# A fused two-layer attention and FFN kernel: the third norm moved into the down products, queries for four sequences at once, the second attention in another order

## The reference

```python
x = x + L0_xattn(layernorm(x), ctx, ctx, ...)   # gated attention, 4 heads
x = x + L0_ffn(layernorm(x), w_gate, w_up, w_down)  # quantized FFN, 768 wide
x = x + L1_xattn(layernorm(x), ctx, ctx, w_q, b_q, w_k, b_k, w_v, b_v, w_o, b_o)  # 16 heads of 16
x = x + L1_ffn(layernorm(x), w_router, wi, wo)  # top-2 of 8 experts, 1024 wide, capacity 160
```

```python
q = (query @ w_q.T + b_q);  k, v likewise from ctx
scores = q @ k.T / sqrt(16)          # per head, 128 x 128
out = softmax(scores) @ v            # per head
out = out @ w_o.T + b_o
```

## Time and profile before

| | us |
|---|---|
| median of 3 runs | 653.67 |
| lowest and highest | 650.80, 655.14 |
| the profiled execution, its own time | 650.85 |
| its span | 649.1 |
| PE busy in it | 547.4 (84%) |
| DVE busy | 385.5 (59%) |
| ACT busy | 297.5 (46%) |
| POOL busy | 153.2 (24%) |

### The profile page before, as it was taken

How to read it: one execution, slowest core, us unless ns; L and a number is a source line. 1 busy time by engine, 2 the same in 40 slices (tenths; PEclk the granted TensorE clock), 3 DMA queues, 4 the chain that set the end, 5 groups by cost and what they waited for, 6 DMA issues and landing times.

```text
span 649.1 us, 10190 instructions
## 1 busy us (share of the span) xinstructions
PE 547.4 (84%) x3542; PEld 385.3 (59%) x3542; DVE 385.5 (59%) x931; ACT 297.5 (46%) x584; POOL 153.2 (24%) x218
## 2 busy tenths in 40 slices
PE   1869999899899103999799999988489999999994
PEld 1548866644344003788576666656277777777773
DVE  5666789644599798676677777774723213332111
ACT  1536587433699696000487777773211222112220
POOL 2725442000000000000322222202014443444531
PEclk9979999899899755999999999998789999999998
DMA  7800000000000000700000000001303544545310
GB/s 232 264 1 3 2 0 1 2 0 1 0 0 0 1 1 0 259 0 0 1 2 2 33 8 28 23 13 55 112 22 111 186 129 152 178 122 186 116 51 21
DMA packets 30152, 37.57 MB, mean 58 GB/s; under 512 B 6560, under 2 KB 25888, under 8 KB 30112
## 3 DMA queue, kind: packets, MB, share of 16 engines
q1 hardware_dynamic: 27040, 29.07, 13.6%
q0 software_dynamic: 3072, 7.95, 4.1%
HBM read 30.14 MB, written 6.88 MB: 57 GB/s over the span
## 4 chain that ended last, share of the span: by engine, by line
PE 67%; DVE 15%; ACT 9%; issue 5%; SPq 1%; DMA 1%; DVEq 0%; POOL 0%; ACTq 0%; POOLq 0%
PE pA L1631 11%; PE pB L1649 9%; PE pC L1441 6%; PE pC L1482 4%; PE pB L1491 3%; PE pA L1476 3%; PE pB L1464 3%; PE pB L1551 3%; PE pA L1403 3%; ACT arena L570 2%; PE pC L1642 2%; PE pC L1315 2%; PE pC L1403 2%; PE pB L1403 2%; DVE arena L1039 2%
## 5 line engine op out<-in xcount | busy, mean ns | idle before, releaser
L1631 PE MATMUL pA<-arena 128*128 128x320 f32 x256 | 72.2, 436 | 0.9 <-ACT arena L733 0.9
L452 POOL TENSOR_TENSOR arena<-KT,par 128x256 f32<-128x256 f32 x32 | 18.9, 613 | 221.5 <-PE pC L1441 201.5
L740 ACT ACTIVATE arena<-pA 128x320 f32<-128x320 f32 x64 | 28.0, 437 | 73.8 <-PE pA L1631 73.8
L1631 PEld LDWEIGHTS pA<-arena 128*128 128x128 f32 x256 | 48.0, 190 | 19.5 <-ACT arena L733 1.0
L1649 PE MATMUL pB<-arena 128*128 128x256 f32 x256 | 59.3, 385 | 0.0
L1649 PEld LDWEIGHTS pB<-arena 128*128 128x128 f32 x256 | 47.4, 190 | 9.4 <-issue 3.1
L972 DVE TENSOR_REDUCE am<-arena 128x1 f32<-128x512 f32 (+1 forms) x48 | 32.0, 680 | 23.7 <-ACT arena L607 23.7
L1104 DVE TENSOR_REDUCE rm<-pA 128x16 f32<-128x2048 f32 x16 | 36.7, 2291 | 14.8 <-PE pA L1476 14.8
L1226 PE MATMUL pB<-ident 128*128 128x128 f32 x120 | 18.6, 323 | 31.0 <-DVE arena L1039 31.0
L692 ACT ACTIVATE arena<-pC 128x512 f32<-128x512 f32 x64 | 38.2, 597 | 9.6 <-PE pC L1482 8.5
L1441 PE MATMUL pC<-wdnT,XIT 128*128 128x256 f32 x192 | 41.7, 380 | 0.9 <-DVE XIT L1059 0.9
(11 more groups left out here) (289 smaller groups left out, 1173.8 us busy)
## 6 DMA issues: line engine op xcount, KB each, us to landing
arena<-in_L_ffn_wi SPq DMA_DIRECT2D x8, 1024.0 KB, 5.1
arena<-in_L_ffn_wo SPq DMA_DIRECT2D x8, 1024.0 KB, 6.0
X<-in_x SPq DMA_DIRECT2D x4, 512.0 KB, 5.9
arena<-in_ctx SPq DMA_DIRECT2D x4, 512.0 KB, 5.8
out<-X SPq DMA_DIRECT2D x4, 512.0 KB, 2.9
token_rows<-arena SPq DMA_DIRECT2D x4, 512.0 KB, 4.0
arena<-in_L_ffn_w_up SPq DMA_DIRECT2D x1, 768.0 KB, 9.2
arena<-in_L_ffn_w_gate SPq DMA_DIRECT2D x1, 768.0 KB, 10.7
```

Of the source, the lines that this page charges most:

```text
L740: nc.scalar.activation(HT[:, u, f, :], ps[2 + f % 2][:, 0:ROWS], ACT.Relu).then_inc(s["h_relu"], 1)
L1631: last = mm(ps[2 + f % 2][:, 0:ROWS], WI[:, u, k, f * P:(f + 1) * P], XET[:, u, k, :], start=(k == 0), stop=(k == KD - 1))
```

## The change

- **Norm in the down stage.** DVE runs moments for sequences 0 to 7 at its turn t = 9 of the down stage, for 8 to 11 at t = 13, and norms two sequences a turn from t = 10 on, into the four buffers that `pair` names. The last four sequences' moments are cut in two: `variances` behind the stage, `inverse_roots` in the attention.
- **Queries for four.** `c_turn(p)` transposes a pair of sequences into one bank; `c_query(c, e)` makes half e of the queries of four sequences in two matmuls of 512 columns; `q_out(c, e)` puts them into XIT, where all queries stay. c_turn 0 to 3 and the first queries stand among the down products, the rest ahead of and in the attention's first turns. OT moves out of XIT.
- **New order.** In PE's turn t come a_out(t-3), o_turn(t-2), turn_3(t-1), scores1(t+1), turn_0(t), a_turn(t-2), values(t-1) in one block, turn_1(t), turn_2(t). Transposes 0, 1 and o_turn use one bank of pC, 2 and 3 the other. ACT and DVE are written out in matching orders, and the keep_busy of this stage is gone.
- POOL's `split_keys` starts when o_int has done eight sequences, and the tables that POOL writes to XIT wait for the last scores.

```diff
+        XC4 = [F3[:, o:o + 1024].rearrange("p (k n) -> p k n", k=KD) for o in (512, 2048)]
...
-        OT = tiles(XIT, 0)
+        OT = view(HALF, 2, FT, P)
...
-        BANK_OF = (1, 1, 0, 1)
+        BANK_OF = (1, 1, 0, 0)
+        QUERY_BANK = ((2, 3), (6, 7), (4, 4), (4, 6))
+        TURN_BANK = (4, 5, 4, 5, 4, 5, 6, 6)
...
                 if isinstance(b, int) and b == 0:
-                    pool.wait_ge(s["down_done"], NB)
+                    pool.wait_ge(s["oi_ready"], 8)
...
+            pool.wait_ge(s["scores"], NB)
...
+            def xt_copy(p):
+                act.wait_ge(s["c_tr"], p + 1)
+                c = p // 2
+                if c >= 2:
+                    act.wait_ge(s["c_q"], 2 * c - 2)
+                nc.scalar.activation(XC4[c % 2][:, :, (p % 2) * 2 * P:(p % 2 + 1) * 2 * P], ps[TURN_BANK[p]][:, :].rearrange("p (k n) -> p k n", k=KD), ACT.Copy).then_inc(s["c_xt"], 1)
+            def q_out(c, e):
+                act.wait_ge(s["c_q"], 2 * c + e + 1)
+                nc.scalar.activation(XITv[:, e, 512 * c:512 * c + 512], ps[QUERY_BANK[c][e]][:, :], ACT.Identity, scale=0.25, bias=bq[:, e:e + 1]).then_inc(s["qt_ready"], 1)
+            rsqrt(3, 8)
+            xt_copy(0)
+            xt_copy(1)
+            rsqrt(4, 4, 8)
+            xt_copy(2)
+            q_out(0, 0)
+            q_out(0, 1)
+            xt_copy(3)
...
             def pt_copy(b, u, g):
+                if g == 0:
+                    free_after(act, s["pv_done"], b)
                 act.wait_ge(s["pt_tr"], b * 4 + g + 1)
...
-            steps(act, NB, [(exps_first, 2), (os_copy, 3), (exps_last, 2), (xt_copy, 0), (pt_first, 2), (q_out, 0), (pt_second, 2), (at_copy, 3), (pt_rest, 2)])
-            rsqrt(4, NB)
+            xt_copy(4)
+            xt_copy(5)
+            q_out(1, 0)
+            q_out(1, 1)
+            rsqrt(5, 4, 12)
+            for t in range(NB + 4):
+                x, y, o, a = t, t - 1, t - 2, t - 3
+                if a >= 0 and a < NB:
+                    at_copy(a, a % 2)
+                if t == 2:
+                    q_out(2, 1)
+                if 0 <= y < NB:
+                    pt_copy(y, y % 2, 0)
+                if t == 1:
+                    q_out(2, 0)
+                if t == 2:
+                    xt_copy(6)
+                if t == 4:
+                    xt_copy(7)
+                if 0 <= o < NB:
+                    os_copy(o, o % 2)
+                if t == 5:
+                    q_out(3, 1)
+                if 0 <= y < NB:
+                    pt_copy(y, y % 2, 1)
+                    pt_copy(y, y % 2, 2)
+                if x < NB:
+                    exps(x, x % 2, 0)
+                if 0 <= y < NB:
+                    pt_copy(y, y % 2, 3)
+                if x < NB:
+                    exps(x, x % 2, 1)
+                if t == 4:
+                    q_out(3, 0)
+            rsqrt(6, NB)
...
+            def norm3(p):
+                if p >= 2:
+                    dve.wait_ge(s["c_tr"], p - 1)
+                for r in range(2):
+                    normed(pair(p, r), 2 * p + r).then_inc(s["xn3"], 1)
+            V_.tensor_scalar(bq[:, :], bq[:, :], 0.25, None, ALU.mult)
+            for t in range(NB + 2):
+                if t < NB:
+                    o_int(t, t % 2)
+                if 1 <= t < NB + 1:
+                    residual(t - 1, (t - 1) % 2)
+                if t >= 2:
+                    stats3(t - 2)
+                if t == 9:
+                    dve.wait_ge(s["row_stats"], NB + 8)
+                    moments(3, 8, D)
+                if t == 13:
+                    dve.wait_ge(s["row_stats"], NB + 12)
+                    moments(4, 4, D, None, 8)
+                if 10 <= t < NB:
+                    norm3(t - 10)
             dve.wait_ge(s["row_stats"], 2 * NB)
-            V_.tensor_scalar(bq[:, :], bq[:, :], 0.25, None, ALU.mult)
-            moments(3, NB, D)
-            def add_attn(b, u, h):
+            variances(4, D, None, 12)
...
-                free_after(dve, s["pv_done"], b)
                 for e in range(2):
+                    if b >= 2:
+                        dve.wait_ge(s["pt_tr"], 4 * (b - 2) + 2 * e + 2)
...
-            steps(dve, NB, [(row_max, 2), (attn_out, 4), (less_max, 2), (norm3, 0), (add_attn, 4), (stats4, 5)])
+            for t in range(NB + 4):
+                if 0 <= t - 4 < NB:
+                    stats4(t - 4)
+                if t == 1:
+                    inverse_roots(5, 4, None, 12)
+                if t == 2:
+                    norm3(6)
+                    norm3(7)
+                if t < NB:
+                    row_max(t, t % 2)
+                    less_max(t, t % 2)
+                if 0 <= t - 3 < NB:
+                    add_attn(t - 3)
+                if 0 <= t - 2 < NB:
+                    attn_out(t - 2, t % 2)
...
-            steps(pe, NB, [(down, 0)])
-            def c_turn(b, u, h):
-                if b == 0:
-                    keep_busy(ps[5], 12)
-                pe.wait_ge(s["xn3"], b + 1)
-                if isinstance(b, int) and b < 4:
-                    if b >= 1:
-                        pe.wait_ge(s["qt_ready"], b)
-                else:
-                    pe.wait_ge(s["x3_ready"], b - 3)
+            def c_turn(p):
+                pe.wait_ge(s["xn3"], 2 * p + 2)
+                if 2 <= p < 6:
+                    pe.wait_ge(s["c_xt"], p - 1)
                 for k in range(KD):
-                    last = tr(ps[4][:, k * P:(k + 1) * P], T[:, u, k * P:(k + 1) * P], ident[:, :])
+                    for r in range(2):
+                        last = tr(ps[TURN_BANK[p]][:, (2 * k + r) * P:(2 * k + r + 1) * P], pair(p, r)[:, k * P:(k + 1) * P], ident[:, :])
                 last.then_inc(s["c_tr"], 1)
-            def c_query(b, u, h):
-                pe.wait_ge(s["c_xt"], b + 1)
-                for e in range(KD):
-                    for k in range(KD):
-                        last = mm(ps[4][:, (2 + e) * P:(3 + e) * P], wT[0][:, k, e * P:(e + 1) * P], XCT[:, u, k, :], start=(k == 0), stop=(k == KD - 1))
+            def c_query(c, e):
+                pe.wait_ge(s["c_xt"], 2 * c + 2)
+                for k in range(KD):
+                    last = mm(ps[QUERY_BANK[c][e]][:, :], wT[0][:, k, e * P:(e + 1) * P], XC4[c % 2][:, k, :], start=(k == 0), stop=(k == KD - 1))
                 last.then_inc(s["c_q"], 1)
-            def scores1(b, u, h):
-                if b < 2:
-                    keep_busy(ps[5], (2, 6)[b])
-                pe.wait_ge(s["qt_ready"], b + 1)
+            for b in range(NB):
+                down(b, b % 2)
+                if 11 <= b < 15:
+                    c_turn(b - 11)
+                if b == 13:
+                    c_query(0, 0)
+                    c_query(0, 1)
...
-            def turn_0(b, u, h):
+            def turn_0(b, u):
                 pe.wait_ge(s["p_ready"], 2 * b + 1)
-                if b >= 1:
-                    pe.wait_ge(s["pt_ready"], 4 * b)
+                if b == 0:
+                    pe.wait_ge(s["qt_ready"], 4)
+                elif b == 1:
+                    pe.wait_ge(s["pt_ready"], 2)
+                else:
+                    pe.wait_ge(s["ao_ready"], b - 1)
                 turn_group(b, u, 0)
...
-            def turn_2(b, u, h):
+            def turn_2(b, u):
                 pe.wait_ge(s["p_ready"], 2 * b + 2)
                 if b >= 1:
-                    pe.wait_ge(s["ao_ready"], b)
+                    pe.wait_ge(s["pt_ready"], 4 * b)
+                if b in (1, 3):
+                    pe.wait_ge(s["c_xt"], 7 if b == 1 else 8)
+                if b == 4:
+                    pe.wait_ge(s["qt_ready"], 8)
                 turn_group(b, u, 2)
-            def turn_3(b, u, h):
-                pe.wait_ge(s["pt_ready"], 4 * b + 2)
+            def turn_3(b, u):
+                pe.wait_ge(s["pt_ready"], 4 * b + 3)
                 turn_group(b, u, 3)
...
+            def values(b, u):
                 if b >= 1:
                     pe.wait_ge(s["os_ready"], b)
-                value_group(b, u, 0)
-            def values_1(b, u, h):
-                value_group(b, u, 1)
-            def values_2(b, u, h):
-                value_group(b, u, 2)
-            def values_3(b, u, h):
-                value_group(b, u, 3).then_inc(s["pv_done"], 1)
-            def a_turn(b, u, h):
+                else:
+                    pe.wait_ge(s["c_xt"], 6)
+                for g in range(4):
+                    last = value_group(b, u, g)
+                last.then_inc(s["pv_done"], 1)
...
+            def o_turn(b, u):
+                pe.wait_ge(s["os_ready"], b + 1)
+                if b + 1 < NB:
+                    pe.wait_ge(s["pt_ready"], 4 * (b + 1) + 2)
+                else:
+                    pe.wait_ge(s["ao_ready"], b)
+                for t in range(4):
...
                 pe.wait_ge(s["ao_ready"], b + 1)
-                if b + 3 >= NB:
+                if b >= 1:
```

(46 more changed lines are left out.)

127 lines of the change are left out of this document (52 added, 75 removed).

## The result

The changed kernel takes 630.31 us (median of 4 runs, 629.59 to 631.85), the one before 652.23 beside it (4 runs): a ratio of 0.9654 with an interval of 0.9623 to 0.9684. Two later sets of runs of the same kernel gave 630.47 and 630.17. The forecast was 640.4 and the range 633.0 to 651.0: the direction was right and the gain much larger. The profiled execution took 631.85 (span 630.1) against 650.85 (span 649.1), 19.0 less.

What follows compares the result with a forecast made beforehand. The prediction took PE to bound the kernel. Loop -14.7, down stage and head +1.2 and tail +0.2 summed to -13.3 us, from the median 653.67 to a forecast of 640.4, range 633 to 651.

Steps and rivals of the forecast that it cites:

- the gate rows: Queries for four: priced by the gate product's rows, four 512-column matmuls in 3.43 us, so 1.72 a c_query call.
- rival (e): Queries: long products are cheap, four 512-column matmuls taking 1.6 us in place of 3.43; total 633 us; chance 0.03.
- In the loop: Second attention's turns: without c_turn, queries and waits a turn falls from 7.96 to 6.49 us; loop gain 14.7 us.
- Rival (d): More gain: no stall at t = 9 and turns 0.2 us shorter from fewer matmul-kind changes; 636 us; chance 0.1.
- two waits: Attention turn: PE's waits for xt_copy at turn_0 (0.16 us) and pt_copy at the first value group (0.09) go.
- PE stays the bound, with 0.4 to 0.6 us to spare: Steady attention turn: all waits on DVE and ACT are met, so PE's 6.49 us of work sets its length.
- The signs: Steady attention turn: PE's sum would read 6.4 to 6.6 us, with under 0.15 idle.
- The tail: From scores(15) to the window's end: 19.7 us against 19.5 before, a loss of 0.2.
- The down stage: Down stage and head: added transposes, queries and a 1.65 us idle lengthen the stage, the head vanishes; net loss 1.2 us.
- POOL: Down stage: some 3.8 us of POOL work beside DVE could cost PE up to 2 us; taken as 0.
- rival (a): Attention turns: DVE becomes the bound, POOL or hand-overs adding 1.2 us to its 6.0; 649 us, half of it 645; chance 0.2.
- rival (b): Attention turns: gain hidden as DVE and POOL exclude each other wholly, 7.9 us a turn; 654 us; chance 0.04.

Runs made afterwards that it cites:

- e6: Changed kernel plus six-fold rows of PE matmul patterns, each kind alone and in turns with another, ahead of the fourth norm's transposes; 672.38 us in one run.

## Why the prediction was right in direction and wrong in size

**What held.** PE bounded the loop before, and the work that the change takes out of the turn came back as time. The long products cost what the gate rows said: eight records, which are four matmuls, took 3.44 (304.94 to 308.38), and one call of two matmuls 1.72 (347.17 to 348.89), against 3.43 in the earlier trace rows. The Trainium skill's ratio of 1.6 for 512 columns against 128 (page "TensorE: Matmul & The Clock Gate", section "Back-to-back issue gap") would have given 1.6 us for the four, an estimate with the 1.00 us of the four at 128 columns; the trace disagrees, and rival (e) falls. The way from scores(0) to scores(1) was 6.82 us (forecast 6.8), from there to scores(2) 6.11 (6.1).

**The step that failed** is "In the loop": "What is left is 7.96 - 0.22 - 1.00 = 6.74", and from it 6.49. It carried each remaining piece over at its pitch among its old neighbours, the values at 4 x 0.35 and a_out at 1.07. Pitches depend on neighbours: five changes between full array and strips fewer, at 0.13 to 0.16 (the patterns), are 0.65 to 0.8 us, and PE needs 5.68, 0.81 less. Rival (d) named this ("fewer changes between kinds of matmul are left") and gave it 0.2. The mechanism was there and mis-sized by a factor of four. The step also took off 0.25 for two waits, where the window of that turn has only 0.13 of PE idle (7.83 of 7.96): counted from PE's work, 7.83 - 1.22 = 6.61, the turn lost 0.93. The changes are 0.65 to 0.8 of that; the 0.13 to 0.28 left over no run prices. The earlier trace rows have no two value groups in a row, so the pitch inside a block had no row at all; it wanted a bound from below, and got only rival (d)'s 0.2. A group took 0.35 apart, and the block of four takes 1.03.

**What followed from it.** "PE stays the bound, with 0.4 to 0.6 us to spare" is then false: with PE at 5.68 the loop scores, row_max, less_max, which the same paragraph put at 6.0 and which measures 6.03, comes last. The signs that the prediction named for a steady turn, a sum of 6.4 to 6.6 with under 0.15 idle, read 5.75 and 0.29. The loop's sum was 6.05 + 6.5 + 7.05 + 10.6 + nine of 6.49; it measured 6.03, 6.03, 6.10, 10.07 and nine of 6.03. The 6.10 is 5.68 of PE and a c_turn of 0.43, the 10.07 are 5.68, 3.44, 0.78 of waiting for q_out (forecast 0.65) and a remainder of 0.17. That is 6.1 of the miss. Without the DVE loop the miss would have been larger still.

**The tail** has for the most part the same cause: pieces of PE that the forecast took too long. From 409.98, turn 14 took 3.84 up to its a_out (forecast 4.4), turn 15 5.95 (6.0, of which 1.31 waiting for attn_out(13) and not 0.6), the pieces from there to the end of the last o_turn 5.3 (5.95), and the last a_out 1.13 to the end of its record (1.4: before it had run at a lower granted clock, 0.72). The last chain of attn_out, a_turn and at_copy was 1.8 (1.9). Together 17.99 against 19.7.

**The down stage** had its mechanism right, with small errors either way: four c_turn cost 1.76 and not 2.1; the idle ahead of down(10) was 1.78 and not 1.65; 0.40 came ahead of down(11), which the forecast took at 0 and kept 2 for; and each of the two idles cost another 0.25: a product's record ends 0.16 after the point where the next would have started (2.75 long at a pitch of 2.59), and one that starts behind an idle is 0.1 longer (2.86). scores(0) came 49.97 after the start and not 49.4. The assumption that the second moments cost nothing held. That the first could be had for nothing (rival (d)'s other half) did not: in three other placements of DVE's work the idle time only moved.

**POOL.** In the down stage POOL's add_bo and split_keys ran beside o_int and norm3 from 293.57, and the two parts of o_int took 1.94 in place of 1.17; taking POOL away took all of that back, 0.76 on PE's path. The Trainium skill, page "SBUF — State Buffer", section "SBUF: two separate sides", has the port shared and locked; the trace agrees that they hold each other up, with 0.77 us more in o_int and 0.26 in norm3 beside 3.36 of POOL, not the whole of it, and POOL's split_keys(1) took 1.81 in place of 1.19. In the turns row_max takes 2.29 beside POOL's 1.87 us, as before; the last one of the kernel before (428.86) had no POOL operation beside it and took 2.29 too. So rival (a) in its form (POOL and hand-overs add 1.2 to DVE's loop) and rival (b) did not come. DVE's row_max and less_max did come into the bound, in the loop with scores, but at 6.03, as a limit to the gain and not as a loss.

**Still open:** the 1.25 us more ahead of the down stage in the profiled execution. They go with the clock, which is not shown to be the whole cause: the two profiles that came latest to that stage (264.55 and 264.83) have a granted clock of 0.80 from 25 to 50 us and 0.86 or 0.87 from 150 to 175, where the kernel before has 0.86 and 0.93. And the prices of e6 tell what a change costs, not which part of the engine's work takes it.

## What to carry to other kernels

When an order is changed, don't add up old pitches: take each kind of piece from the longest unbroken row of its kind and price each change of kind by itself. Then put the next limit beside the sum: a loop through one set of banks (scores, row_max, less_max) that had 1.9 us to spare before was the bound after. Where an engine is full, moving its queue about moves the wait with it; in these runs only the work taken from beside it, POOL's, shortened the stage by more than 0.2 us.

## What the runs showed that was not expected

- A change between matmuls of the full array and matmuls on strips of 32 rows or 32 columns costs 0.13 to 0.16 us; between transposes and 256-column products of the full array nothing.
- Order alone, with the same instructions, was worth 6.1 us of 654, and the reverse of it in the new kernel cost 14 us, more than half of them a new wait.
- An idle of PE in the down stage costs about 0.25 us on top of itself: 0.16 are the tail of the last record, 0.1 the longer first product.
- A reduction over 64 of 128 keys takes 1.22 us against 2.29. The softmax is the same for any value subtracted that keeps the exponential in range, so what that version gives up is the guarantee and not the formula; it was fastest, 626.63, and is no equal replacement.
